# A two-layer graph attention on one core: edge steps taken in pairs, with one unbroken row of gathers for each pair

## What is computed

```python
h = (h_in @ W).reshape(n, 4, 64)
alpha_s, alpha_d = sum(h * a_s, -1), sum(h * a_d, -1)
e = leaky_relu(alpha_s[src] + alpha_d[dst], 0.2)
m = segment_max(e, dst);  ex = exp(e - m[dst])
alpha = ex / segment_sum(ex, dst)[dst]
out = segment_sum(h[src] * alpha[:, :, None], dst) + b
```

## Time and profile before

| | us |
|---|---|
| three executions, lowest / median / highest | 5359.52 / 5388.16 / 5414.55 |
| the profiled execution | 5359.35 |
| its span, first to last instruction | 5357.5 |
| DVE busy in the span | 3477.3 (65%) |
| POOL busy | 3356.7 (63%) |
| PE busy | 2843.2 (53%) |
| ACT busy | 2231.7 (42%) |

### The profile page before, as it was taken

How to read it: one execution, slowest core, us unless ns; L and a number is a source line. 1 busy time by engine, 2 the same in 40 slices (tenths; PEclk the granted TensorE clock), 3 DMA queues, 4 the chain that set the end, 5 groups by cost and what they waited for, 6 DMA issues and landing times. The chain is left out here.

```text
span 5357.5 us, 63241 instructions
## 1 busy us (share of the span) xinstructions
PE 2843.2 (53%) x9790; PEld 1922.3 (36%) x9790; DVE 3477.3 (65%) x12389; ACT 2231.7 (42%) x6943; POOL 3356.7 (63%) x3189
## 2 busy tenths in 40 slices
PE   6455555555555555555544555455545555454455
PEld 5333333333334333333323333333333333332333
DVE  5466666666666666666655767666756766666676
ACT  4244444444444444444433444334434444443344
POOL 3466666666666666666646666666566666666664
PEclk9777777777777777777766777677767777777777
DMA  6444444444444444444434444444444444444443
GB/s 213 122 117 119 121 119 116 116 117 118 120 115 122 117 115 120 116 119 117 116 87 117 136 130 132 122 130 131 124 123 130 130 132 134 130 127 126 125 131 95
DMA packets 342320, 662.83 MB, mean 124 GB/s; under 512 B 99107, under 2 KB 211531, under 8 KB 341915
## 3 DMA queue, kind: packets, MB, share of 16 engines
q0 software_dynamic: 151056, 429.17, 30.1%
q1 hardware_dynamic: 128952, 172.16, 10.6%
q10 hardware_dynamic: 62018, 59.05, 3.2%
HBM read 597.44 MB, written 62.65 MB: 123 GB/s over the span
## 5 line engine op out<-in xcount | busy, mean ns | idle before, releaser
L505 POOL DMA_INDIRECT rows_all<-table,edge x3136 | 3315.7, 1057 | 1934.6 <-issue 1527.0
L1142 PE MATMUL bank<-rows_all,onehot 128*128 128x264 f32 x6272 | 1982.1, 471 | 62.8 <-remote 42.6
L1142 PEld LDWEIGHTS bank<-rows_all,onehot 128*128 128x128 f32 x6272 | 1426.8, 238 | 431.9 <-issue 144.0
L1116 PE MATMUL bank<-onehotT,logit_p 128*128 128x448 bf16 x896 | 369.7, 567 | 1346.5 <-issue 1008.9
L576 ACT ACTIVATE rows_all<-rows_all 128x64 f32<-128x64 f32 x3584 | 876.6, 333 | 12.8 <-issue 12.6
L871 DVE TENSOR_TENSOR rows_all<-rows_all 128x768 f32<-128x768 f32 (+1 forms) x672 | 694.6, 1034 | 0.0
L1116 PEld LDWEIGHTS bank<-onehotT,logit_p 128*128 128x128 bf16 x896 | 97.1, 127 | 1555.1 <-issue 1404.3
L1152 PE MATMUL bank<-total,heir 128*128 128x264 f32 x448 | 187.0, 505 | 736.8 <-DVE heir L994 301.0
L589 ACT ACTIVATE share<-node_d 128x8 f32<-128x8 f32 x224 | 46.7, 209 | 1115.3 <-DVE node_d L954 713.6
L612 ACT ACT_TABLE_LOAD x224 | 287.4, 1283 | 525.9 <-issue 416.7
L893 DVE TENSOR_TENSOR onehot<-iota_f,dloc 128x1792 f32<-128x1792 f32 x224 | 453.9, 2027 | 0.9 <-remote 0.9
(11 more groups left out here) (165 smaller groups left out, 3538.0 us busy)
## 6 DMA issues: line engine op xcount, KB each, us to landing
dst_b<-dst_row SPq DMA_DIRECT2D x224, 448.0 KB
rows_all<-table,edge POOLq DMA_INDIRECT x3136
self_row<-table SPq DMA_DIRECT2D x224, 132.0 KB
table<-row ACTq DMA_DIRECT2D x113, 132.0 KB
x_row<-in_x_dram SPq DMA_DIRECT2D x112, 128.0 KB
out_dram<-y_out ACTq DMA_DIRECT2D x112, 128.0 KB
act_pad<-act_o ACTq DMA_DIRECT2D x112, 128.0 KB
table<-row ACTq DMA_DIRECT2D x24, 528.0 KB, 3.8
```

The costliest lines, as they stand in the source:

```text
L505: nc.gpsimd.indirect_dma_start(out=G[u][:, j, :], out_offset=None, in_=table[L][0:N, :], in_offset=bass.IndirectOffsetOnAxis(ap=index[:, j ...
L1116: last = nc.tensor.matmul(bank[0][:, 0:SLOTS * SQ], logit_p[:, q * P:(q + 1) * P], of[:, q], start=(q == 0), stop=(q == QUADS - 1))
L1142: last = nc.tensor.matmul(bank[3 + t.half][:, 0:ROW], onehot[t.half][:, j, :], G[t.u][:, j, :], start=(j == 0), stop=(j == SLOTS - 1))
```

## The change

Steps are taken in pairs. There are two sets of pair buffers in place of four sets of step buffers, the small operations on DVE cover both steps of a pair in one instruction, and every loop turn is two pairs. The roles are now `known`, `landed`, `finished`, `multiplied`, `stored` (from newest to oldest pair).

- POOL issues 28 gathers in a row, and waits only between pairs: for the nodes' logits on edges of the pair before (`ad_done`), for the sum of the pair before that (`sum_done`) and for the edge data.
- SP loads the edge data first in its turn and no longer behind the window's own rows of another step; it takes over the running sum: `hand_over` stores `total` to main memory, waits, and reads the heir's row back into `old_row`, once for each step.
- PE's transposes of the ends and its `heir` matmul are gone. DVE transposes in blocks of 32 by 32 (`ends_t`, `carry_t`) and copies quarters.
- The numbers 0 to 127, the edges' weights and the bias lie in a PSUM bank, so the long DVE operations read one input from SBUF and one from PSUM. ACT writes the exponentials to PSUM and copies them into the rows.
- DVE weighs 20 of 28 slots in four parts, ACT 8 in two parts, and the first step's part comes first.

```diff
-    PARTS = [(0, 4), (4, 7), (7, 10), (10, SLOTS)]
-    DVE_PARTS = 3
+    PARTS = [(0, 4), (4, 9), (9, SLOTS), (SLOTS, 20), (20, 24), (24, PS)]
+    DVE_PARTS = 4
...
+        edge_w = bank[2][:, 0:PS * H]
+        numbers = bank[2][:, P:2 * P]
+        bias_p = bank[2][:, 2 * P:2 * P + HC]
...
+            def load_edges(t):
+
+                for k in range(2):
+                    sp.wait_ge(s["onehot_ready"], t.step(k, 2))
+                    nc.sync.sem_inc(loads_begun, 1)
+                    chunk = sp.value_load(steps_i[0:1, T_CHUNK, bass.ds(t.first + k, 1)], min_val=0, max_val=CHUNKS)
+                    sp.dma_start(edge[t.h][:, k].rearrange("p f t -> p (f t)"),
+                                 edges[bass.ds(chunk, 1)].rearrange("o p w -> (o p) w")).then_inc(s["edge_landed"][t.h], 16)
...
+            def hand_over(t, k):
+
+                sp.wait_ge(s["total_ready"], t.step(k, 0))
+                nc.sync.sem_inc(hands_begun, 1)
+                sp.dma_start(hand[k][0:P, :], total[:, k].rearrange("p h c -> p (h c)")).then_inc(s["hand_stored"][k], 16)
+                heir = sp.value_load(steps_i[0:1, T_HEIR, bass.ds(t.first + k, 1)], min_val=0, max_val=P)
+                sp.wait_ge(s["hand_stored"][k], t.k * 16 + 16)
+                nc.sync.sem_inc(hands_begun, 1)
+                sp.dma_start(old_row[0:1, 1 - k], hand[k][bass.ds(heir, 1), :]).then_inc(s["old_landed"][1 - k], 16)
...
+            def sp_body(stored_, multiplied, finished, landed, known_):
+                if known_:
+                    load_edges(known_)
+                    load_nodes(known_)
+                if finished:
+                    load_inputs(finished)
+                    hand_over(finished, 0)
+                if known_:
+                    load_own(known_, 0)
+                    load_own(known_, 1)
+                if finished:
+                    hand_over(finished, 1)
...
-                    for u in range(NB):
-                        t = Step(pool, L, r, rounds_, u, counts)
-                        pool.wait_ge(s["sum_done"], t.done(4))
-                        pool.wait_ge(s["edge_landed"][u], t.landed(16))
+                    for v in range(PAIRS):
+                        t = Pair(pool, L, r, rounds_, v, counts)
+
+                        pool.wait_ge(s["ad_done"], t.done(1))
+                        pool.wait_ge(s["sum_done"], t.done(2))
+                        pool.wait_ge(s["edge_landed"][v], t.landed(32))
                         nc.gpsimd.sem_inc(gathers_begun, 1)
-                        index = edge[u][:, E_SRC, :].bitcast(I32)
-                        for j in range(SLOTS):
-                            if j == SLOTS // 2:
-
-                                pool.wait_ge(s["rowT_done"], t.done(2))
-                                nc.gpsimd.sem_inc(gathers_begun, 1)
-                            nc.gpsimd.indirect_dma_start(
-                                out=G[u][:, j, :], out_offset=None, in_=table[L][0:N, :],
-                                in_offset=bass.IndirectOffsetOnAxis(ap=index[:, j:j + 1], axis=0)).then_inc(s["landed"][u], 16)
+                        for k in range(2):
+                            index = edge[v][:, k, E_SRC, :].bitcast(I32)
+                            for j in range(SLOTS):
+                                nc.gpsimd.indirect_dma_start(
+                                    out=G[v][:, k * SLOTS + j, :], out_offset=None, in_=table[L][0:N, :],
+                                    in_offset=bass.IndirectOffsetOnAxis(ap=index[:, j:j + 1], axis=0)).then_inc(s["landed"][2 * v + k], 16)
 
...
             def exponentials(t):
+
                 act.wait_ge(s["fall_ready"], t.done(0))
-                nc.scalar.activation(G4[t.u][:, :, :, C].rearrange("p t h -> p h t"), fall[:], ACT.Exp).then_inc(s["w_ready"], 1)
+                nc.scalar.activation(edge_w.rearrange("p (s t h) -> p s h t", h=H, s=2), fall[:], ACT.Exp).then_inc(s["w_ready"], 1)
+                act.wait_ge(s["w_ready"], t.done(0))
+                nc.scalar.activation(G4[t.h][:, :, :, C], edge_w.rearrange("p (t h) -> p t h", h=H), ACT.Copy).then_inc(s["wcol_ready"], 1)
 
...
+            def act_body(stored_, multiplied, finished, landed, known_):
+                if multiplied:
+                    move_actT(multiplied)
+                if stored_:
+                    move_rows_on(stored_)
+                    store_rows(stored_, 0)
+                if finished:
+                    shares(finished, 0)
+                if stored_:
+                    store_rows(stored_, 1)
+                if multiplied:
+                    store_outputs(multiplied, 0)
+                if landed:
+                    exponentials(landed)
+                    weigh_last(landed, DVE_PARTS)
+                if multiplied:
+                    store_outputs(multiplied, 1)
+                if finished:
+                    shares(finished, 1)
+                if landed:
+                    weigh_last(landed, DVE_PARTS + 1)
+                if finished:
+                    gelu(finished)
 
             pipeline(nc.scalar, act_body)
 
...
+            def ends_to_rows(t):
                 dve.wait_ge(s["ahead_ready"], t.done(0))
                 dve.wait_ge(s["behind_ready"], t.done(0))
+                dve.wait_ge(s["ends_t_ready"], t.done(1))
+                nc.vector.tensor_copy(ends[:, 0:2, 0:H], ahead[:, :, SLOTS - 1].rearrange("p (s h) -> p s h", h=H))
+                nc.vector.tensor_copy(ends[:, 2:4, 0:H], behind[:, :, 0].rearrange("p (s h) -> p s h", h=H)).then_inc(s["ends_ready"], 1)
                 dve.wait_ge(s["known_ready"], t.done(1))
                 nc.vector.tensor_tensor(run_max[:], ahead[:], behind[:], ALU.max).then_inc(s["run_ready"], 1)
+                dve.wait_ge(s["carry_ready"], t.done(1))
...
+                nc.vector.transpose(ends_t[:].rearrange("p b w -> p (b w)"), ends[:].rearrange("p b w -> p (b w)")).then_inc(s["ends_t_ready"], 1)
...
+                for q in range(QUADS):
+                    last = nc.vector.tensor_copy(rows_h[:, :, q * SQ:(q + 1) * SQ], ends_t[q * SQ:q * SQ + H, :, :])
+                last.then_inc(s["rows_h_ready"], 1)
...
+                for q in range(QUADS):
+                    last = nc.vector.tensor_tensor(carry[q * SQ:q * SQ + H].rearrange("h (a s) i -> h a s i", s=2), run[:, q], m[:, q], ALU.add)
+                last.then_inc(s["carry_ready"], 1)
+                dve.wait_ge(s["carry_ready"], t.done(0))
+                dve.wait_ge(s["reach_ready"], t.step(1, 1))
+                nc.vector.transpose(carry_t[:].rearrange("p b w -> p (b w)"), carry[:].rearrange("p b w -> p (b w)")).then_inc(s["carry_t_ready"], 1)
...
+            def one_hots_of_edges(t, k):
+                dve.wait_ge(s["dloc_ready"], t.step(k, 0))
+                dve.wait_ge(s["sum_done"], t.done(1))
+                nc.vector.tensor_tensor(onehot[:, k], wide(numbers, 1, SLOTS), wide(dloc[:, k], 2, P), ALU.is_equal
+                                        ).then_inc(s["onehot_ready"], 1)
+
+            def weigh(t, nth):
+                t0, t1 = PARTS[nth]
+                rows = G[t.h][:, t0:t1, :].rearrange("p t (h c) -> p (t h) c", h=H)
+                nc.vector.tensor_tensor(rows[:, :, 0:C], rows[:, :, 0:C], wide(edge_w[:, t0 * H:t1 * H], 2, C), ALU.mult
+                                        ).then_inc(s["weighted"][nth], 1)
...
+            def dve_body(stored_, multiplied, finished, landed, known_):
+                if multiplied:
+                    residual(multiplied)
+                if finished:
+                    maxima_of_nodes(finished)
+                    node_shares(finished, 0)
+                if landed:
+                    logits_of_edges(landed)
+                if finished:
+                    node_totals(finished, 0)
+                if landed:
+                    scan_runs(landed)
+                    ends_to_rows(landed)
+                    scan_partitions(landed)
+                if landed:
+                    carries_back(landed)
+                    falls(landed)
+                    places_of_edges(landed)
+                    one_hots_of_edges(landed, 0)
+                    for nth in range(DVE_PARTS - 1):
+                        weigh(landed, nth)
+                if finished:
+                    node_shares(finished, 1)
+                if landed:
+                    one_hots_of_edges(landed, 1)
+                if finished:
+                    node_totals(finished, 1)
+                if landed:
+                    weigh(landed, DVE_PARTS - 1)
+                if finished:
+                    node_means(finished)
+                if known_:
+                    if not landed:
+                        load_bias(known_)
+                    one_hots_of_nodes(known_)
+                    logit_parts(known_)
...
+            def pe_body(stored_, multiplied, finished, landed, known_):
+                if multiplied:
```

(8 more changed lines are left out.)

765 lines of the change are left out of this document (384 added, 381 removed).

## The result

The changed kernel took 5603.36 us (median of 4 runs, 5599.18 to 5610.86) against 5380.25 us for the kernel before on the same chip: 1.041 times as long, 95% interval 1.0352 to 1.0467. The forecast was 5,010 us with a range of 4,560 to 5,560, so the sign was wrong too. But the experiments show that this is one of two answers: on another chip the same two kernels stand at 0.922.

What follows compares the result with a forecast made beforehand. Bound by 224 step periods, with pauses between POOL's gathers and DVE's work and waits. A pair takes 28.0 + 8.0 + 2.5 + 3.3 + 0.2 = 42.0 us against 45.3, giving 5,010 us, range 4,560 to 5,560.

Steps and rivals of the forecast that it cites:

- The period formula: Whole kernel: profiled time is 369 + 110 T us, T being the time of a pair, forecast at 42.0 us.
- DVE's work: DVE's busy time a pair: fewer, wider operations bring it from 29.9 to 28.0 us, bounds 26.7 and 29.9.
- The mean gather: POOL's gathers: a mean near 0.95 us, from 1.067, would show the effect of the constants in PSUM.
- `reach`, `runs` and `dloc`: DVE's waits behind PE's small transposes and the edge data: 774.3 us removed, 6.9 us a pair.
- The eight hops of the new scan chain: DVE's new waits for a neighbour instruction: taken as nothing, up to 10 us a pair if all are slow.
- The wait for the exponential: DVE's weighing now directly follows `fall` and waits for ACT: 2.5 us a pair added, between 1.2 and 5.
- The wait for the logits' matmul: DVE waits for PE's eight matmuls of the logits on edges: 3.3 us a pair added, between 2.3 and 6.
- The hand-over: The running sum's way through main memory by SP: mostly hidden, 0.2 us a pair on the mean.
- The idle time goes from 15.4 to 8.0: DVE's idle us a pair, after removing its waits and half the logit parts' chain, before the added waits.
- Slower: SP becomes the bound: Rival: SP's longer queue, 40 instructions at 1.2 us, makes a pair 48 us, 5,649 us; 22 in 100 with other slower ways.
- POOL is the bound after all: Rival: POOL's 35 to 38.3 us a pair decide, T = 36.5 us, 4,384 us; 12 in 100.

Runs made afterwards that it cites:

- e4: Kernel after without the hand-over through main memory, its semaphore raised at once: 5518.4 us, 1.0291 of before.
- c1: Kernel after, unchanged, run again on a chip without slow steps: 4295.87 us, 0.9218 of before.
- c8: Kernel before, steps one by one, with the numbers and a copy of the edges' weights in PSUM, chip without slow steps: 4232.85 us, 0.9092 of before.
- e1: Kernel after without POOL's wait for `ad_done` of the pair before: 5711.31 us, 1.0666 of before.
- e8: Kernel before with 32 increments of an unused semaphore a step on PE, chip without slow steps: 4659.3 us, 1.0002 of before.
- the sixth set: Runs of c10 and c11 on a chip where before took 5385.84 us; its table gives slow SP register instructions by time since the row began.
- e2: Kernel after with eight memsets on POOL as a break in the middle of a pair's row of gathers: 5496.32 us, 1.0241 of before.
- c11: The program of c8, unchanged, on a chip with slow steps: 5545.15 us, 1.0307 of before.
- e3: Kernel after with 64 increments of an unused semaphore on PE ahead of a pair's sum: 5829.33 us, 1.0844 of before.
- c10: The program of c8 with plain loads from fixed places instead of gathers by index, before at 5385.84 us: 3991.8 us, 0.742 of before.

## Why the prediction was wrong

**Where the steps came out.** The period formula held: (5603.2 - 369) / 110 = 47.6 us a pair against 47.56 in the pair shown, and 47.19 and 47.46 on the mean of the two layers. DVE's work was forecast at 28.0 us; 0.606 of 47.6 is 28.8. The mean gather was forecast near 0.95 and is 0.962. `reach`, `runs` and `dloc` are gone from the waits, 774 us, as forecast. The eight hops of the new scan chain, which I left to the high end, stay quick (39 us of idle time in all, from L1027 to L1064): they stand early in the row, where DVE is busy 16.07 of 17.24 us.

**Terms that were mis-sized.** The wait for the exponential was to be 2.5 us a pair (280 us); L1101 shows 44.0 and 12.9 us, 0.5 a pair. The wait for the logits' matmul was to be 3.3 (370 us); L991 shows 23.0, 0.2 a pair. The hand-over was to be 0.2 and cost 0.8 (e4). Together these are 4.5 us too much, so without the step that failed the forecast would have been lower still.

**The step that failed** is "The idle time goes from 15.4 to 8.0". It took the waits that were not removed as fixed, and they were not. DVE's idle time is 47.6 - 28.8 = 18.8 us a pair. What filled it is the wait for the pair's sum (4.3 us a pair) and for the gelu (2.4), and behind them the whole end of the pair, which POOL's `ad_done` waits for: 1020.5 us, 9.1 us a pair. In the pair shown that is PE and ACT in slow steps. It is so for most of the whole: the same kernel on a chip without them (c1) waits 195.0 us for the sum in place of 481.5, and 12.3 for `ad_done`. I had the slow steps before me, on DVE in the earlier trace rows and on SP in the earlier trace rows, and treated them as a property of those hops and of that queue. The earlier trace rows holds a sign for PE too: 1008.9 us of `issue` ahead of the logits' matmuls. In c8, the nearest program without slow steps, 799.1 of the 800.4 us there end with DVE's work. In the earlier trace rows I even read that in a row of 28 gathers DVE falls from 85% to 65%, and charged it to DVE's waits. What I should have asked is which other engine's instructions would stand late in a row once all rows are 28 long, and at 1.40 us each what the 56 matmuls of a pair's sum, each with its weight load, then cost.

**The rivals.** "Slower: SP becomes the bound" gave the right region (5,649 us) by the wrong mechanism: without the hand-over the kernel still loses 2.9%, and 87 of POOL's waits end with PE's matmul (1020.5 us), 21 between pairs with SP's data (270 us). Its part that is right is that SP's slow steps come next: when `ad_done` was removed, the edge data took over (e1). "POOL is the bound after all", 4,384 us with 12 in 100, is what the kernel does on a chip without slow steps: 4,296 us. Its argument, that the mean gather decides once nothing else is late, was complete; I gave it little because slow steps were in every row that I read.

**What the gains and losses belong to.**

| | chips with slow steps | chips without |
|---|---|---|
| before | 1 (5,377 to 5,386 us) | 1 (4,655 to 4,663 us) |
| constants in PSUM alone | 1.031 | 0.909 |
| pairs alone | not tried | 1.039 |
| both: the kernel after | 1.041 | 0.922 |

The Trainium skill, "SBUF — State Buffer", section "Who interferes with whom", says that a DVE instruction with two SBUF inputs contends with a GpSimd instruction that reads SBUF. The traces of both kinds of chip agree: no gather of over 1.5 us is left in the kernel after, where the kernel before has 269 and, with e8's increments on a chip without slow steps, 464. That shorter gathers can make a kernel slower is in no row of before.

**What stays open.** Why shorter gathers lengthen the gaps on the chips with slow steps is in part argued. The reading that fits: slow steps grow dense while POOL issues gathers without a break, and long gathers and pauses act as breaks. For it stand the table of the sixth set, its split by long gathers, and e2, whose added pause gave 107 us. These are counts over traces in which the instructions near a long gather are also others of the program; no run changed the gathers' length and nothing else on such a chip. Against its being the whole: in c11 SP's slow steps number 1,267, before 1,187, hardly more, and e3 shows that the number of instructions taken counts too. What in the chip makes a step slow is not known. Whether the kinds belong to the chip or to what else it does at that hour isn't known either: each of the six sets was all of one kind, from its first run to its last. And pairs alone, and the kernel after with plain loads, weren't run on a chip with slow steps.

## What to carry to other kernels

Where a trace shows engines with their operands ready that take instructions at 0.7 or 1.4 us each beside GpSimd's gathers by index, don't take the waits that it names as prices: taking one away can move the wait on (e1), and making the gathers denser can cost more than it gives. Measure such a change on more than one chip, since the sign can turn (0.922 and 1.041 here). And take a change with two ideas in it apart before judging it: here the constants in PSUM carried all of the gain on the chips without slow steps, and the pairs cost 1.5% on top.

## What the runs showed of the hardware

- Different Trainium2 chips ran the same program at two speeds: before took 5,380 us or 4,658 us (1.155 times), c8 took 5,545 or 4,233 us (1.31 times), with the same mean gather (0.960 us) at both.
- On the slower kind, beside GpSimd's gathers by index, many of SP's register instructions take 0.70 us and some 1.40, where c8's take 0.02 to 0.18 us on the other kind (its loads into registers 0.26 to 0.74); late in a row PE's matmuls and weight loads come one in 1.40 us, ACT's and DVE's instructions wait about as long. It grows with the time since the row began (in the kernel after 5% of SP's instructions in the first 5 us, 83% behind 20 us) and lasts to some 4 us after the last gather (1537.13 to 1541.55).
- Plain DMAs on the same queue with the same 429.17 MB don't do that: c10 took 3,992 us on the slower kind of chip.
- A DVE instruction with two operands in SBUF makes gathers beside it longer: mean 1.097 us with the constants in SBUF, 0.960 with them in PSUM, in otherwise the same program (e8 and c8), and over 3,136 gathers that is 430 us. (e8 also has its 32 increments on PE, which took no time there.)
